# Moving the first pairs' x parts, queries and context turns in a fused perceiver layer

## The reference

```python
x = x + xattn(layernorm(x), ctx, ctx, ...)   # this part is changed
x = x + attn(layernorm(x), ...)              # small attention along the batch axis
x = x + ffn(layernorm(x), ...)               # 16 experts, top 2, and a shared expert

# xattn: x is (32, 64, 256), ctx is (32, 1601, 256)
q = query @ Wq + bq;  k = ctx @ Wk + bk;  v = ctx @ Wv + bv
probs = softmax(q @ k.T)
result = probs @ v
y = result + query;  return (y - mean) * rsqrt(var + 1e-5) * gamma + beta
```

## Time and profile before

| | us |
|---|---|
| median of 3 runs (531.1 to 534.37) | 531.81 |
| the profiled execution's own time | 533.65 |
| its span, first to last instruction | 531.9 |
| PE busy / DVE busy in the span | 497.1 / 399.8 |
| cross attention, to the last `project` | about 278 |

### The profile page before, as it was taken

The page is one execution under the profiler, slowest core; times in us unless marked ns, Lnnn a source line. Parts: engine busy times, 40 slices in busy tenths (PEclk is TensorE's granted clock), DMA queues, the critical chain, the costliest instruction groups (busy, mean ns, idle before and its releaser), DMA issues.

```text
span 531.9 us, 14446 instructions
## 1 busy us (share of the span) xinstructions
PE 497.1 (93%) x5012; PEld 347.7 (65%) x5013; DVE 399.8 (75%) x1080; ACT 200.0 (38%) x617; POOL 198.1 (37%) x314
## 2 busy tenths in 40 slices
PE   7998999999999999999989999999998979999990
PEld 6665656656666666666655667766754658888860
DVE  3799699999899999899663488898775515555764
ACT  2343413433223333332312466665431035555510
POOL 4000412212221122112221667676776605666640
PEclk9999999999999999999999999999998979999996
DMA  7999579877998788885314899810122235555747
GB/s 280 362 359 265 185 266 304 259 201 251 296 309 281 269 275 273 259 269 204 98 41 128 264 291 310 251 52 2 41 80 91 90 99 150 159 155 154 223 116 221
DMA packets 67604, 108.83 MB, mean 205 GB/s; under 512 B 8371, under 2 KB 49381, under 8 KB 67560
## 3 DMA queue, kind: packets, MB, share of 16 engines
q1 hardware_dynamic: 61144, 97.83, 58.9%
q0 software_dynamic: 3792, 8.43, 4.5%
q10 hardware_dynamic: 2624, 1.97, 1.2%
HBM read 85.31 MB, written 24.85 MB: 207 GB/s over the span
## 4 chain that ended last, share of the span: by engine, by line
PE 71%; DVE 9%; DMA 8%; POOL 5%; issue 4%; ACT 1%; SPq 1%; POOLq 0%; DVEq 0%; ACTq 0%
PE banks L1135 15%; PE banks L1159 15%; PE banks L1541 8%; DMA ring<-in_ctx_dram 4%; POOL rows_by_expert L752 4%; PE banks L1553 4%; PE banks L1147 3%; DVE ctxT L1663 3%; PE banks L1172 3%; PE banks L1094 2%; PE banks L1535 2%; PE banks L1268 2%; PE banks L1320 2%; PE banks L1180 2%; PE banks L1275 2%
## 5 line engine op out<-in xcount | busy, mean ns | idle before, releaser
L1663 DVE STREAM_TRANSPOSE ctxT<-ring 128x832 f32<-128x832 f32 x128 | 121.7, 1008 | 4.4 <-DMA ring<-in_ctx_dram 4.4
L1135 PE MATMUL banks<-ctxT,qT_all 32*64 32x416 f32 (+2 forms) x2048 | 93.8, 498 | 1.6 <-issue 0.9
L1159 PE MATMUL banks<-ring,prob 128*64 128x256 f32 (+1 forms) x832 | 93.6, 381 | 0.7 <-ACT prob L864 0.7
L1159 PEld LDWEIGHTS banks<-ring,prob 128*64 128x64 f32 (+1 forms) x832 | 58.6, 137 | 31.5 <-issue 4.2
L1135 PEld LDWEIGHTS banks<-ctxT,qT_all 32*64 32x64 f32 x2048 | 56.8, 131 | 30.3 <-issue 13.0
L663 POOL TENSOR_TENSOR var<-mv,eps 128x1 f32<-128x1 f32 x32 | 6.3, 196 | 167.7 <-DVE mv L1708 115.6
L786 POOL DMA_INDIRECT expert_out<-prob,dest x47 | 46.2, 984 | 41.7 <-DVE prob L2124 26.1
L877 ACT ACTIVATE prob<-banks,negmax 128x416 f32<-128x416 f32 (+2 forms) x80 | 41.1, 531 | 30.2 <-DVE negmax L1685 30.2
L1541 PE MATMUL banks<-ring,ctxT 128*128 x188 | 50.7, 394 | 0.1
L699 POOL TENSOR_TENSOR ctxT<-ctxT,k_mask 128x1088 f32<-128x1088 f32 x16 | 33.1, 2068 | 25.3 <-ACT ctxT L955 25.3
L864 ACT COPY prob<-banks 128x512 f32<-128x512 f32 x64 | 27.6, 514 | 38.3 <-PE banks L1147 38.2
(11 more groups left out here) (271 smaller groups left out, 940.0 us busy)
## 6 DMA issues: line engine op xcount, KB each, us to landing
ring<-in_ctx_dram SPq DMA_DIRECT2D x48, 1024.0 KB
qT_all<-q_by_pair SPq DMA_DIRECT2D x56, 128.0 KB, 8.9
rows_by_expert<-blank SPq DMA_DIRECT2D x8, 774.0 KB, 5.9
ctxT<-rows_by_expert SPq DMA_DIRECT2D x47, 129.0 KB, 2.1
mid<-stage SPq DMA_DIRECT2D x31, 128.0 KB, 2.3
ring<-in_ctx_dram SPq DMA_DIRECT2D x16, 130.0 KB
ctxT<-mid SPq DMA_DIRECT2D x16, 128.0 KB, 3.7
qT_all<-mid SPq DMA_DIRECT2D x16, 128.0 KB, 3.8
```

What stands on the lines that cost most here:

```text
L1135: last = pe.matmul(S[a][64 * b:64 * b + 64, 0:KW[a]], q_rep[mine, r, c, 64 * b:64 * b + 64], ctxT[mine, c, b, 0:KW[a]], start=c == 0, stop ...
L1159: last = pe.matmul(U[64 * b:64 * b + 64, 0:D], probT[0:rows, k, 64 * b:64 * b + 64], ring[0:rows, r, b, k, :], start=k == 0, stop=k == KT)
L1663: dve.transpose(ctxT[:, c].rearrange("p b (k j) -> p (b k) j", j=Q), ring[:, r].rearrange("p b k c -> p (b k) c")[:, :, columns(c):columns ...
```

## The change

1. **Two x parts at once.** ACT's queue now issues x parts 0 and 1 (pairs 0 to 3); part 1 is taken off SP's queue, where it stood behind pair 0's context. DVE computes the statistics of both parts and norms both at the start; PE and ACT turn both before the bias matmuls.
2. **Direct queries one pair at a time.** `queries_direct(0)` and its placing stand ahead of the first scores; `queries_direct(1)` stands behind `scores(0)` on PE, and its placing ahead of `exps(0)` on ACT. The matmuls have 128 columns instead of 256, and there are twice as many. The eight filler matmuls behind `queries_of(0)` are gone.
3. **The first context turned as it arrives.** The first two parts of pair 0's context have a semaphore of their own, `ctx_first`. When they are there, DVE turns their 256 columns of each of two batch entries for blocks 0 to 3, and the rest (160 each) when all is there; blocks 4 to 7 are turned whole as before.
4. **Later chunks a turn later.** `queries_of(1)` moves from ahead of `turn_probs(1)` into turn 2, and with it the rows and queries of chunks 2 and 3 one turn on each; x parts 3 and 4 likewise. `store_q(1)` is issued by ACT behind `turn(2)`. The transposes of chunk 1 stay behind `weigh(0)`, and the second part of `turn_probs(1)` waits for ACT's copies of them. `query_blocks(0)` moves behind `turned_out(0)`.
5. The dots are spread otherwise (1, 3, 2, 3, 3 instead of 2, 0, 3, 7), and one more turn of PE and three of DVE are written out ahead of the loops.

Its core:

```diff
         sp.wait_ge(tails_ready, RING)
-        load(0, 0)
-        load_x(1)
+        for g in range(len(KPARTS)):
+            load_part(0, 0, g, ctx_first if g < 2 else None)
+        sp.sem_inc(ctx_loaded[0], 32)
         load_x(2)
...
     @block.scalar
-        act.dma_start(x_all[:, 0:DIRECT, :], x_rows[:, 0:DIRECT, :]).then_inc(x_loaded[0], 16)
+        for n in range(2):
+            part = slice(*XPARTS[n])
+            act.dma_start(x_all[:, part, :], x_rows[:, part, :]).then_inc(x_loaded[n], 16)
...
         first_rows_turned()
+        next_rows_turned()
...
-        queries_placed()
-        next_rows_turned()
+        queries_placed(0)
+        queries_placed(1)
...
         exps(0)
+        turned_out(0)
         query_blocks(0)
-        turned_out(0)
         exps(1)
         rows_turned(1)
-        query_blocks(1)
+        turn(2, queries=1)
         store_q(1)
-        turn(2, rows=2)
-        turn(3, queries=2)
+        turn(3, rows=2)
+        turn(4, queries=2)
         store_q(2)
...
     @block.tensor
         scores(0, 0, 0, True)
-        next_queries_turned()
+        queries_direct(1)
         queries_of(0)
-        keep_awake(8, T[1])
         turn_probs(0, first=True)
...
         queries_turned(1)
-        queries_of(1)
-        pe.wait_ge(qT_copied, 4)
-        turn_probs(1)
+        turn_probs(1, turned=1)
         pe.wait_ge(weights_loaded, REST_LOADED)
-        turn(2, 2, 0, back3=False, rows=2)
-        turn(3, 0, 1, queries=2)
-        turn(4, 1, 1, rows=3)
-        turn(5, 2, 1, queries=3)
+        turn(2, 2, 0, back3=False, queries=1)
+        turn(3, 0, 1, rows=2)
+        turn(4, 1, 1, queries=2)
+        turn(5, 2, 1, rows=3)
+        turn(6, 0, 2, queries=3)
...
     @block.vector
+        arrived = KPARTS[1][-1] + 1
+        dve.wait_ge(ctx_first, 32)
+        for c in range(SOONER):
+            chunks_turned(c, 0, arrived)
+        dve.wait_ge(ctx_loaded[0], 64)
+        for c in range(SOONER):
+            chunks_turned(c, arrived, KT + 1).then_inc(block_ready, 1)
+        for c in range(SOONER, BLOCKS):
             block_turned(0, 0, c, 0)
-        x_statistics(1)
...
-        turn(2, 2, 0, back3=False, also=(4, 6))
-        turn(3, 0, 1, of_x=4)
-        turn(4, 1, 1, also=(6, 9))
-        turn(5, 2, 1, also=(9, PAIRS))
+        turn(2, 2, 0, back3=False, also=(4, 5), of_x=3)
+        turn(3, 0, 1, also=(5, 8))
+        turn(4, 1, 1, also=(8, 10), of_x=4)
+        turn(5, 2, 1, also=(10, 13))
+        turn(6, 0, 2, also=(13, PAIRS))
```

More of the change, by code:

```diff
@@ L32, in perceiver_layer @@
     EARLY = 5
+    SOONER = 4
     KPARTS = [range(lo, min(lo + KG, KT + 1)) for lo in range(0, KT + 1, KG)]
@@ L501, in _ @@
                 follow(i, i % RING)
-            for m in range(2):
-                sp.wait_ge(q_stored[m], 2 * 16 * QUADS)
+            sp.wait_ge(q_stored[0], 2 * 16 * QUADS)
             for i in range(8, RING + 7):
                 follow(i, i % RING)
+            sp.wait_ge(q_stored[1], 2 * 16 * QUADS)
             with sp.Fori(0, (PAIRS - RING - 7) // RING) as it:
@@ L655, in x_deviation @@
                 pool.tensor_tensor(x_rstd[:, part], x_var[:, part], m_half[:, part], ALU.pow).then_inc(x_rstd_ready, 1)
-            for n in range(4):
+            for n in range(3):
                 x_deviation(n)
@@ L896, in _ @@
             exps(0)
+            turned_out(0)
             query_blocks(0)
-            turned_out(0)
             exps(1)
             rows_turned(1)
-            query_blocks(1)
+            turn(2, queries=1)
             store_q(1)
-            turn(2, rows=2)
-            turn(3, queries=2)
+            turn(3, rows=2)
+            turn(4, queries=2)
             store_q(2)
-            turn(4, rows=3)
-            turn(5, queries=3)
+            turn(5, rows=3)
+            turn(6, queries=3)
             store_q(3)
-            with act.Fori(6, PAIRS) as i:
+            with act.Fori(7, PAIRS) as i:
                 turn(i)
@@ L1119, in _ @@
                       bqk_of[:, :, :].rearrange("p a d -> p (a d)"), start=True, stop=True).then_inc(wqk_done, 1)
-            pe.wait_ge(xnT_copied, 2)
-            for c in range(BLOCKS):
-                queries_direct(c)
+            pe.wait_ge(xnT_copied, 4)
+            queries_direct(0)
             def scores(i, r, round_, direct=False, cs=range(BLOCKS)):
@@ L1137, in scores, with turn_probs @@
                     last.then_inc(block_used, 1)
-            def turn_probs(i, first=False):
+            def turn_probs(i, first=False, turned=None):
                 pe.wait_ge(exp_done, (i + 1) * len(EXPS))
                 for g, ks in enumerate(KPARTS):
+                    if g == 1 and turned:
+                        pe.wait_ge(xnT_copied, 2 * turned + 4)
                     if g == len(KPARTS) - 1 and not first:
```

60 lines of the change are left out of this document (36 added, 24 removed).

## The result

| | median us | runs |
|---|---|---|
| before, on the same chip | 532.48 (531.1 to 535.64) | 6 |
| changed | 536.85 (535.51 to 539.09) | 6 |

The ratio of changed to before is 1.0068 [1.0039, 1.0097]: about 3.6 us slower, where 2.1 us faster were forecast. The three together say some 0.5%, 2.7 us, which is still within 1%, but outside the range that was given. The ratios leave out runs in a slower state, 3 of 12 of e1, 5 of 12 of e2, 3 of 12 of e3 and 1 of 6 of e5, and the profiled executions of e1 and e2 are of that kind, so that e2's ratio rests on seven runs.

A forecast was written before the change was run, and what follows sets the result against it. PE, busy 497.1 of 531.9 us, was taken as the bound. A 4.0 us net lead, 2.5 spent by pair 4's scores, plus pair 8's vanished wait, gave 2.1 less: median 531.8 to 529.7, range 527.0 to 533.2.

The forecast's parts named there:

- the wait of 0.9 us for pair 4's context: Turn 3: SP goes on at 62, context issued 63.8, landed 75.8; DVE wants it at 74.9, so waits 0.9.
- What is late next: Forecast step on late transfers: DVE waits 1.1 us for pair 3's context and 0.9 for pair 4's.
- rival C: Pair 4's context held behind SP's wait for stores under load: lands 79.7, 533.6 us (531.8 to 534.5), chance 0.22.
- From there both kernels run the same turns: From pair 8's scores on, PE's work decides in both kernels; the sum stays 2.1 us less.
- S(8): Start of pair 8's scores on PE: forecast 149.5 against 151.6 before.
- The lead at E(2): End of pair 2's scores: 53.1 against 60.8, 7.7 us ahead, 4.0 net of the 3.7 owed for `queries_of(1)`.
- S(2): Start of pair 2's scores on PE: forecast 47.3, within 1 us, against 54.19 before.
- S(1): Start of pair 1's scores on PE: forecast 31.8, after `turn_probs(0)` starts at 30.1.
- lost at once: Sign of error: pair 2's queries, forecast back at about 47, come after 49; every us there is lost.
- Pair 8's wait goes: Turn 7's wait of 0.9 us for pair 8's context vanishes because turn 6 is 3.7 longer; worth about 1 us.
- the last block at 22.0: Pair 0's context on DVE: last block turned at 22.0, against 23.7 before.
- Rival D: Head: early context turns bring nothing, parts landing together or short turns costing full price; 530.0 to 531.0, chance 0.06.

The follow-up runs named there:

- e1: Changed kernel with part 4 (later chunks a turn later) undone, so the head only, against the kernel before: ratio 0.9986 [0.9955, 1.0017].
- e2: Kernel before with part 4 (later chunks a turn later) alone: ratio to before 1.0043 [0.9999, 1.0086].
- e3: Changed kernel with pair 4's context issued ahead of SP's wait for chunk 1's stores: ratio to before 0.9993 [0.9960, 1.0026].
- e5: As e3, and each later context also issued ahead of the store of an older result: ratio to before 1.0272 [1.0224, 1.032].
- e8: The changed kernel measured again, nothing altered: ratio to before 1.0029 [1.0002, 1.0056].
- e9: The changed kernel measured once more, beside three other kernels: ratio to before 1.0057 [1.0031, 1.0082].
- e10: The same edit as e3, pair 4's context first in the changed kernel, measured again: ratio to before 1.0023 [0.9999, 1.0046].
- e15: Changed kernel without the context transfers of pairs 3 to 8, old data used again (results wrong): ratio to before 0.9957 [0.9935, 0.9980].
- e16: Kernel before without the context transfers of pairs 3 to 8, old data used again (results wrong): ratio to before 0.9987 [0.9959, 1.0015].
- e11: As e10, with pair 3's context also issued ahead of the load of its queries: ratio to before 1.0015 [0.9989, 1.0041].
- e12: The head-only kernel of e1 measured again: ratio to before 0.9996 [0.9977, 1.0015].
- e14: Changed kernel with pair 4's context held until pair 3's scores were read, and filler matmuls in PE's waits: 544.42 us, one run.
- e7: Kernel before with each context issued ahead of an older result's store on SP's queue: ratio to before 1.0306 [1.027, 1.0341].

## Why the prediction was wrong

- **The step that failed** is the wait of 0.9 us for pair 4's context in "What is late next". Two terms of it were too small. The landing was taken as 12 us from the first issue and took 14.7 (13.3 and 15.2 in e8 and e9). And SP goes on at 64.93 instead of 62, which is of this one profile (62.5 and 62.8 in e8 and e9): turn 2 starts later, since pair 2's queries came back late, and `scores(2)` took 1.3 us more at half clock. The context landed at 81.4, not 75.8; DVE's wait was 3.6 (0.9 and 2.9 in e8 and e9). The prediction had such a wait in rival C, and gave it 0.22 because of an idle queue. The stores were indeed as quick as on an idle queue (2.3 us), so C's own condition, stores under load, did not hold either; it was the issue time and the landing that decided. That SP's order costs is measured (e9 against e10).
- **"From there both kernels run the same turns"** failed too, and e8, where the wait at pair 4 was the forecast's 0.9, shows it best. It is 1.1 us ahead of the kernel before at S(8) (150.5 against 151.6; the forecast was 149.5) and 1.3 behind at S(12) (211.2 against 209.9), at full clock all the while. A wait for pair 9's context (1.19) is in it, and a `scores(10)` of 6.8 us; what lengthened that one is not shown.
- **The lead at E(2)** was 1.8 net (e15 against e16), not 4.0. S(2) came 1.4 later than 47.3 even there: 0.8 is the wait for pair 2's queries, and the rest came with the head (S(0) 0.7 and S(1) 0.9 late). The other 0.8 was in the E(2) of before: 60.8 in that one profile, 60.0 in e16. In the changed kernel's first profile those queries left 0.6 later than forecast, and their way back took 5.7 to 7.6 us where it took 3.4 to 4.0 before; what slowed it is not shown. The prediction had named this as what would make it wrong, "lost at once", and it was.
- **"Pair 8's wait goes"** was an error of logic. The issue of pair 8's context is gated by `weigh(5)`, which moves with the turns; a longer turn 6 helps only what is gated by an earlier one. In the changed kernel DVE waits 1.0 there too (0.5 in e9, none in e8, which waits at pair 9). In the same way pairs 5 to 9 each meet the same distance between slot freed and block wanted: the prediction had looked for a wait at pairs 3 and 4 only, and e11 shows them at 3, 4, 6 and 8. This is the likely reason why no order on SP that was tried kept the rest of the lead.
- **Right**: the last block at 22.0; S(1) within 0.7 us of its forecast; a net gain of the order of work alone of about 2 us (1.7 measured in e15 and e16, but those have no transfers to pay); the size of the effect, under 1%, though not its sign. Rival D's condition did not hold: the early turns came in time, yet the head alone is worth nothing that 21 runs can show. `exps(0)` starts when ACT has placed pair 1's direct queries and not behind the last block, as the prediction said.
- **The pages.** A short turn took 2.48 / 4 = 0.62 us from start to start for 512 columns and 0.42 for 320, where scaling by columns had given 0.58 and 0.36. The Trainium skill (VectorE: DVE Perf Modes, "The TRN2 errata") gives a VectorE instruction from SBUF to SBUF 58 cycles beside one for each element at 0.96 GHz, an estimated 0.59 and 0.39 us, and 0.93 for 832 columns. The trace agrees that there is a fixed part; it lies 0.03 above for the short turns and 0.01 above for 832 columns (0.94). On the queues the trace fits what the Trainium skill (DMA: Bandwidth & Descriptors, "Issuing engines are not separate DMA queues") says, that transfers of different issuing engines interleave on the same 16 DMA engines: with x part 1 on ACT's queue, pair 0's context on SP's landed 0.4 us later (16.6 against 16.2).

Of the forecast's rivals, C came true in its place, SP's queue ahead of pair 4's context. Its time was 533.6, which is 1.8 us above the kernel before; by the ratios the changed kernel is 3.6, 1.5 and 3.0 us above it, so C's size is within the spread of the three. How the loss divides between pair 4's wait, the missing 2.2 us of lead and the waits of later pairs was not measured.

No kernel tried that reads its whole input beats the kernel before by more than its interval: e1 and e12 are its equals, e11 comes close with the changed order.

## What to carry to other kernels

When work is moved so that a stage starts earlier, follow each transfer that the stage will want: from what frees its buffer, through everything ahead of it on the issuing queue, to its landing. If what frees it moves with the work, the distance stays and no lead helps; if it stands behind a wait on another engine's store, the lead is turned into a wait. And measure how much of a lead is there by leaving the transfers out: one pair of such kernels told here what no single profile did. A single profile can show a clock loss of several microseconds (3.7 here) that the average over many runs doesn't have.

## What the runs showed of the hardware

- TensorE's clock was granted at half behind waits of PE of 1.0 (e2, at S(2)), 2.1, 3.5 (e14), 3.6 (e2), 4.0 and 10.9 us, and stayed there while PE worked again: scores of 5.82 us took 7.1 and 7.5 us behind the two short waits and 8.0 to 8.6 behind the others. But a wait of 3.3 us passed at full clock in another execution of the changed kernel, so the length of the wait alone did not decide.
- The same program ended its attention at 279.4, 281.7 and 287.1 us in three profiled executions, and its waits for one transfer were 0.9, 2.9 and 3.6 us. One profile does not size such a wait.
- Two stores of 128 KB issued behind 3.3 MB of context on the same queue took 6.9 to 9.5 us to land (e7) where the median of such stores was 2.3 ahead of it. They held DVE up to 5.7 us at a time, and the order cost the kernel before 3%.
- A context of 3.3 MB took 11.4 to 13.8 us from its last issue to landing where a chain ran over it (before, changed, e8, e9, e11).
